# Mixture of experts in seven products a unit: P1 seeded into P2's bank by ScalarE, a second prefix added into P5's bank by VectorE, both gates read by silu from PSUM, down products in halves

## The reference

```python
# x: (16, 256, 256) float32; 8 routed experts and one shared; D = 256, F = 1024
g = einsum('bsd,edf->ebsf', x, Wg)
u = einsum('bsd,edf->ebsf', x, Wu)
expert_outs = einsum('ebsf,efd->ebsd', silu(g) * u, Wd)
expert_output = einsum('be,ebsd->bsd', probs, expert_outs)
shared = silu(x @ Sg) * (x @ Su) @ Sd
sg = shared_gate[:, None, None]
out = x + (1.0 - sg) * expert_output + sg * shared
```

## Time and profile before

| what | value |
|---|---|
| median of 3 runs | 2184.85 us (2184.4 to 2184.9) |
| the profiled execution's own time | 2184.52 us |
| its span (first to last instruction) | 2182.7 us |
| TensorE busy | 2157.2 us, 99% of the span, 9504 matmuls |
| VectorE busy | 1493.0 us, 68% |
| ScalarE busy | 1532.0 us, 70% |
| GpSimd busy | 1394.3 us, 64% |

### The profile page before, as it was taken

One profiled execution on the slowest core, in us unless ns is written; L12 is line 12 of the kernel. 1 busy time (PEld: TensorE's weight loads), 2 busy tenths in 40 slices (PEclk: granted clock), 3 DMA queues, 4 the chain that ended last, 5 costly groups with the idle time before them and its releaser, 6 DMA issues.

```text
span 2182.7 us, 34606 instructions
## 1 busy us (share of the span) xinstructions
PE 2157.2 (99%) x9504; PEld 1784.5 (82%) x9504; DVE 1493.0 (68%) x2622; ACT 1532.0 (70%) x2622; POOL 1394.3 (64%) x2055
## 2 busy tenths in 40 slices
PE   6999999999999999999999999999999999999998
PEld 5888888888888888888888888888888888888887
DVE  6666666666766666666676666666667666666666
ACT  6777677677777767766776776777677677777765
POOL 8766666666866666666686666666666666666662
PEclk9999999999999999999999999999999999999999
DMA  4111111111211111111121111111112111111110
GB/s 151 52 57 50 50 57 51 50 53 55 71 51 58 50 50 56 52 50 51 57 71 52 58 51 50 53 55 50 50 58 70 52 57 51 50 52 57 50 50 27
DMA packets 44171, 122.22 MB, mean 56 GB/s; under 512 B 4928, under 2 KB 4944, under 8 KB 44128
## 3 DMA queue, kind: packets, MB, share of 16 engines
q1 hardware_dynamic: 44064, 121.65, 18.3%
q0 software_dynamic: 64, 0.07, 0.1%
HBM read 117.51 MB, written 4.19 MB: 56 GB/s over the span
## 4 chain that ended last, share of the span: by engine, by line
PE 98%; DMA 0%; POOL 0%; ACT 0%; DVE 0%; issue 0%; SPq 0%; DVEq 0%; ACTq 0%
PE chain_ps L255 12%; PE down_ps L255 12%; PE chain_ps L257 12%; PE chain_ps L256 12%; PE down_ps L257 12%; PE down_ps L256 12%; PE p_ps L255 6%; PE p_ps L257 6%; PE p_ps L256 6%; PE p_up_ps L255 3%; PE p_up_ps L257 3%; PE p_up_ps L256 3%; DMA w_raw<-w 0%; POOL w_lo L183 0%; POOL w_raw L168 0%
## 5 line engine op out<-in xcount | busy, mean ns | idle before, releaser
L183 POOL TENSOR_TENSOR w_lo<-w_raw,w_hi 128x384 fp32r<-128x384 f32 x864 | 854.6, 1018 | 733.0 <-ACT w_hi L342 733.0
L168 POOL TENSOR_TENSOR w_raw<-w_raw 128x128 f32<-128x128 f32 x1152 | 509.6, 465 | 29.0 <-DMA w_raw<-w 6.4
L255 PE MATMUL chain_ps<-x_hi,w_hi 128*128 128x512 f32 x1152 | 449.1, 390 | 19.4 <-POOL w_lo L183 18.2
L342 ACT CAST w_hi<-w_raw 128x768 fp32r<-128x768 f32 x576 | 388.5, 675 | 86.9 <-PE down_ps L257 80.1
L255 PE MATMUL down_ps<-h_hi,w_hi 128*128 128x512 f32 x1152 | 448.3, 389 | 0.5 <-DVE h_lo L459 0.5
L256 PE MATMUL chain_ps<-x_lo,w_hi 128*128 128x512 f32 x1152 | 448.4, 389 | 0.0
L257 PE MATMUL chain_ps<-x_hi,w_lo 128*128 128x512 f32 x1152 | 448.4, 389 | 0.0
L257 PE MATMUL down_ps<-h_hi,w_lo 128*128 128x512 f32 x1152 | 448.1, 389 | 0.0
L256 PE MATMUL down_ps<-h_lo,w_hi 128*128 128x512 f32 x1152 | 448.1, 389 | 0.0
L363 ACT CAST h_hi<-p_up_ps 128x512 fp32r<-128x512 f32 x288 | 169.0, 587 | 307.0 <-DVE p_up_ps L451 307.0
L474 DVE TENSOR_TENSOR gate<-tap_p,p_up_ps 128x512 f32<-128x512 f32 x288 | 198.0, 687 | 248.6 <-PE p_up_ps L257 248.6
(11 more groups left out here) (46 smaller groups left out, 2852.6 us busy)
## 6 DMA issues: line engine op xcount, KB each, us to landing
w_raw<-w SPq DMA_DIRECT2D x288, 384.0 KB, 3.0
outT<-acc SPq DMA_DIRECT2D x8, 512.0 KB, 4.1
acc<-xT SPq DMA_DIRECT2D x6, 512.0 KB, 9.3
acc<-xT SPq DMA_DIRECT2D x4, 256.0 KB, 6.3
probs_sb<-probs POOLq DMA_DIRECT2D x1, 64.0 KB, 5.1
shared_sb<-shared_gate POOLq DMA_DIRECT2D x1, 8.0 KB, 6.3
```

Source lines behind the costliest of these rows:

```text
L168: nc.gpsimd.tensor_tensor(raw[:, cols(dst, dst)], raw[:, cols(a, a)], raw[:, cols(b, b)], op).then_inc(w_sums, 1)
L183: ins = nc.gpsimd.tensor_tensor(w_lo[:, s, c], w_raw[:, s, c], w_hi[:, s, c].bitcast(F32), ALU.subtract)
L255: nc.tensor.matmul(bank, w_hi[:, s, c], hi, start=start, stop=False, **on)
L342: nc.scalar.copy(w_hi[:, s, c], w_raw[:, s, c]).then_inc(w_hi_done, 1)
```

## The change

- ScalarE no longer copies P1 to SBUF (tap_p1). It copies it from the chain bank into the bank of P2 (now y_ps), and P2 is then accumulated on top by TensorE: the bank holds gate 0. The copy (the seed) waits until h1_lo(n-1) has read the bank, and P6(n) waits for the seed.
- One matmul ahead of all units opens that bank, so that later accumulating matmuls add to what ScalarE writes.
- gate0 and gate1 of VectorE and the tap of U2 are gone. In their place VectorE adds tap_p5 and U2 and writes the sum into P5's bank (now z_ps; `u4`, waits for P6 and the tap of P5), and P3 is accumulated on top: gate 1.
- Both silus read PSUM: silu 0 after P2, silu 1 after P3.
- up_of_1 waits for silu 0 instead of gate0; P5(n) waits for silu 1 of unit n-1.
- TensorE's order is now P4(n-1), P1(n), P5(n), first half of down0(n-2), P6(n), second half of down0(n-2), P2(n), P7(n), P3(n), down1(n-1). P7 waits for u4.
- ScalarE's order is now h1_hi(n-1), h0_hi(n-1), seed(n), tap of P5, weights' hi part 0, silu 0, weights' hi part 1, (casts of x), silu 1.
- VectorE's order is now h0(n-1), h1_lo(n-1), h0_lo(n-1), u4, up_of_1, h1(n), (add).

```diff
...
         warm = sb("warm", [P, 1])
 
         chain_ps = ctx.enter_context(nc.psum_tensor("chain_ps", [P, 2, TOKENS], F32))
-        p2_up1_ps = ctx.enter_context(nc.psum_tensor("p2_up1_ps", [P, TOKENS], F32))
-        p53_ps = ctx.enter_context(nc.psum_tensor("p53_ps", [P, TOKENS], F32))
+        y_ps = ctx.enter_context(nc.psum_tensor("gate0_up1_ps", [P, TOKENS], F32))
+        z_ps = ctx.enter_context(nc.psum_tensor("p5_gate1_ps", [P, TOKENS], F32))
         down_ps = ctx.enter_context(nc.psum_tensor("down_ps", [P, 2, DC, TOKENS], F32))
...
                     pe.wait_ge(x_lo_done, X_FORMS * g + form + 1)
                 return x_hi[:, g % 2, form, :], x_lo[:, g % 2, form, :]
 
-            def down0(k, start, stop):
-                for c in range(DC):
-                    last = product(
-                        down_ps[:, 0, c, :], k % SLOTS, D0 + c, h0_hi[:, k % 2, :], h0_lo[:, k % 2, :], start, stop
-                    )
-                last.then_inc(down_done[0], 1)
-
-            def down1(k, start, stop):
-                for c in range(DC):
-                    last = product(down_ps[:, 1, c, :], k % SLOTS, D0 + c, h1_hi[:], h1_lo[:], start, stop)
-                last.then_inc(down_done[1], 1)
+            def down0(k, c, start, stop):
+                last = product(
+                    down_ps[:, 0, c, :], k % SLOTS, D0 + c, h0_hi[:, k % 2, :], h0_lo[:, k % 2, :], start, stop
+                )
+                if c == DC - 1:
+                    last.then_inc(down_done[0], 1)
+
+            def down1(k, c, start, stop):
+                last = product(down_ps[:, 1, c, :], k % SLOTS, D0 + c, h1_hi[:], h1_lo[:], start, stop)
+                if c == DC - 1:
+                    last.then_inc(down_done[1], 1)
 
             def p4(g, k, n, first=False):
 
...
                 if not isinstance(n, int) or n > 0:
                     p4(g - 1 if first else g, (k - 1) % CHUNKS, n - 1, first=in_first and k == 1)
 
+                def down0_part(c):
+                    if not isinstance(n, int) or n > 1:
+                        opens = in_first and k == 2
+                        if c == 0:
+                            pe.wait_ge(h_lo_done[0], n - 1)
+                            if opens:
+                                after(pe, added[0], g)
+                        down0((k - 2) % CHUNKS, c, start=opens, stop=in_first and k == 1)
+
+                def down1_both():
+                    if not isinstance(n, int) or n > 0:
+                        pe.wait_ge(h_lo_done[1], n)
+                        opens = in_first and k == 1
+                        if opens:
+                            after(pe, added[1], g)
+                        for c in range(DC):
+                            down1((k - 1) % CHUNKS, c, start=opens, stop=first)
+
                 pe.wait_ge(w_lo_done, n + 1)
                 after(pe, h_lo_done[0], n - 1)
                 product(chain, s, A11, *x_of(g, B11, first), start=True, stop=True).then_inc(p1_done, 1)
-                after(pe, gate1_done, n)
-                product(p53_ps[:], s, S1, *x_of(g, T1, first), start=True, stop=True).then_inc(p5_done, 1)
-                if not isinstance(n, int) or n > 1:
-                    pe.wait_ge(h_lo_done[0], n - 1)
-                    opens = in_first and k == 2
-                    if opens:
-                        after(pe, added[0], g)
-                    down0((k - 2) % CHUNKS, start=opens, stop=in_first and k == 1)
-                pe.wait_ge(p1_tapped, n + 1)
+                after(pe, silu_done[1], n)
+                product(z_ps[:], s, S1, *x_of(g, T1, first), start=True, stop=True).then_inc(p5_done, 1)
+                down0_part(0)
+                pe.wait_ge(p1_seeded, n + 1)
                 product(chain, s, S2, *x_of(g, T2, first), start=False, stop=True, goes_on=True).then_inc(p6_done, 1)
-                after(pe, h_lo_done[1], n)
-                product(p2_up1_ps[:], s, A12, *x_of(g, B21, first), start=True, stop=True).then_inc(p2_done, 1)
-                pe.wait_ge(p5_tapped, n + 1)
-                product(p53_ps[:], s, S4, *x_of(g, B22, first), start=False, stop=True, goes_on=True).then_inc(p3_done, 1)
-                pe.wait_ge(u2_tapped, n + 1)
+                down0_part(1)
+                product(y_ps[:], s, A12, *x_of(g, B21, first), start=False, stop=True, goes_on=True).then_inc(p2_done, 1)
+                pe.wait_ge(u4_done, n + 1)
                 product(chain, s, S3, *x_of(g, T3, first), start=False, stop=True, goes_on=True).then_inc(p7_done, 1)
-                if not isinstance(n, int) or n > 0:
-                    pe.wait_ge(h_lo_done[1], n)
-                    opens = in_first and k == 1
-                    if opens:
-                        after(pe, added[1], g)
-                    down1((k - 1) % CHUNKS, start=opens, stop=first)
-
+                product(z_ps[:], s, S4, *x_of(g, B22, first), start=False, stop=True, goes_on=True).then_inc(p3_done, 1)
+                down1_both()
+
+            pe.wait_ge(x_lo_done, 1)
+            pe.wait_ge(w_lo_done, 1)
+            nc.tensor.matmul(y_ps[:], w_hi[:, 0, 0:P], x_hi[:, 0, B11, :], start=True, stop=True).then_inc(y_opened, 1)
             for g in range(GROUPS):
                 for k in range(CHUNKS):
                     unit(g, 0, k)
...
 
                 if not first:
                     h1_hi_of(n - 1)
+                    h0_hi_of(n - 1, k - 1)
                 act.wait_ge(p1_done, n + 1)
-                after(act, gate0_done, n)
-                nc.scalar.copy(tap_p1[:], chain_ps[:, k % 2, :]).then_inc(p1_tapped, 1)
+                if first:
+                    act.wait_ge(y_opened, 1)
+                after(act, h_lo_done[1], n)
+                nc.scalar.copy(y_ps[:], chain_ps[:, k % 2, :]).then_inc(p1_seeded, 1)
                 act.wait_ge(p5_done, n + 1)
                 after(act, up1_done, n)
-                nc.scalar.copy(tap_p5[:], p53_ps[:]).then_inc(p5_tapped, 1)
-                if not first:
-                    h0_hi_of(n - 1, k - 1)
+                nc.scalar.copy(tap_p5[:], z_ps[:]).then_inc(p5_tapped, 1)
                 if ahead:
                     weight_hi(n + AHEAD, (k + AHEAD) % SLOTS, 0)
-                act.wait_ge(p6_done, n + 1)
-                after(act, gate1_done, n)
-                nc.scalar.copy(tap_u2[:], chain_ps[:, k % 2, :]).then_inc(u2_tapped, 1)
+                act.wait_ge(p2_done, n + 1)
+                after(act, h0_done, n)
+                nc.scalar.activation(silu[:, 0], y_ps[:], ACT.Silu).then_inc(silu_done[0], 1)
                 if ahead:
                     weight_hi(n + AHEAD, (k + AHEAD) % SLOTS, 1)
                 if new_x:
                     for form in X_AT.get(k, ()):
                         x_form_hi(g + 1, form)
-                act.wait_ge(gate0_done, n + 1)
-                after(act, h0_done, n)
-                nc.scalar.activation(silu[:, 0], gate[:, 0], ACT.Silu).then_inc(silu_done[0], 1)
-                act.wait_ge(gate1_done, n + 1)
+                act.wait_ge(p3_done, n + 1)
                 after(act, h1_done, n)
-                nc.scalar.activation(silu[:, 1], gate[:, 1], ACT.Silu).then_inc(silu_done[1], 1)
+                nc.scalar.activation(silu[:, 1], z_ps[:], ACT.Silu).then_inc(silu_done[1], 1)
 
             act.wait_ge(warm_set, 1)
             nc.scalar.activation(warm[:], warm[:], ACT.Silu).then_inc(warmed, 1)
...
             def h1_lo_of(n):
                 dve.wait_ge(h_hi_done[1], n + 1)
                 after(dve, down_done[1], n)
-                nc.vector.tensor_tensor(h1_lo[:], p2_up1_ps[:], h1_hi[:].bitcast(F32), ALU.subtract).then_inc(
+                nc.vector.tensor_tensor(h1_lo[:], y_ps[:], h1_hi[:].bitcast(F32), ALU.subtract).then_inc(
                     h_lo_done[1], 1
                 )
 
-            def gate0(n):
-                dve.wait_ge(p2_done, n + 1)
-                dve.wait_ge(p1_tapped, n + 1)
-                after(dve, silu_done[0], n)
-                nc.vector.tensor_tensor(gate[:, 0], tap_p1[:], p2_up1_ps[:], ALU.add).then_inc(gate0_done, 1)
-
-            def gate1(n):
-                dve.wait_ge(p3_done, n + 1)
-                dve.wait_ge(u2_tapped, n + 1)
-                after(dve, silu_done[1], n)
-                nc.vector.tensor_tensor(gate[:, 1], tap_u2[:], p53_ps[:], ALU.add).then_inc(gate1_done, 1)
+            def u4(n, k):
+                dve.wait_ge(p6_done, n + 1)
+                dve.wait_ge(p5_tapped, n + 1)
+                nc.vector.tensor_tensor(z_ps[:], tap_p5[:], chain_ps[:, k % 2, :], ALU.add).then_inc(u4_done, 1)
 
             def up_of_1(n, k):
                 dve.wait_ge(p7_done, n + 1)
-                dve.wait_ge(p5_tapped, n + 1)
-                dve.wait_ge(gate0_done, n + 1)
-                nc.vector.tensor_tensor(p2_up1_ps[:], tap_p5[:], chain_ps[:, k % 2, :], ALU.add).then_inc(up1_done, 1)
+                dve.wait_ge(silu_done[0], n + 1)
```

(29 more changed lines are left out.)

## The result

| | before | after |
|---|---|---|
| median | 2184.62 us (4 runs) | 2339.45 us (4 runs) |
| the profiled execution's own time | 2184.52 us | 2339.39 us |
| its span | 2182.7 us | 2337.6 us |

The change makes the kernel slower: ratio 1.0708, 95% interval 1.0695 to 1.0721, 154.8 us. Forecast were 2322 us (+138), range 2290 to 2351.

The account below looks back on a forecast made before the run. TensorE, busy 99%, was taken as the bound. P6's wait for the seed (130.0 us), additions (3.2), address price (3.8) and start (1.0) summed to 138.0 on 2184.5: 2322 us, range 2290 to 2351.

Parts of the forecast that it names:

- links 1 to 3 and 6: From P4(n-1): h0 starts at 0.88 us, h1_lo 0.785 later, lasting 0.69; after the seed, ScalarE to TensorE takes 0.05.
- Link 4, VectorE to ScalarE: Hand-over from h1_lo's end on VectorE to the seed's start on ScalarE: 0.03 us.
- Link 5, the seed: The seed's copy on ScalarE, priced like the tap into SBUF: 0.589 us, with bounds 0.48 and 0.69.
- Link 7, the restart: TensorE restarts slowly after P6 was held: 0.14 us more per unit.
- The address price: h0, heading VectorE's queue, starts 0.12 us later once per loop pass for its changed coefficient address: 3.8 us.
- The additions: At changes of group the addition stands between h1 and h0 on VectorE: 6 times 0.54, 3.2 us.
- Start and tail: One opening matmul and less cover for P6 in the second unit: 1 us; the tail 0.
- The covers named: Work said to stay hidden: u4 by 0.4 us, up_of_1 by a us; T is the start of P4(n-1).
- The signs named: Profile after: P6 idle behind the seed, some 0.3 us on weight loads; unit 7.93; P7 not held; TensorE about 95%.
- not slower: Rival at P6's wait for the seed: chain 0.5 us shorter than its rows, so no cost, 2185 us; chance 2%.
- a smaller and a larger stall: Rivals at P6: links overlap at queue distance, 2268 us, 5%; seed at 0.69 and u4 late, 2380 us, 6%.
- The clock: Rival: TensorE's clock falls to its low level; a quarter of the units would give 2800 us; chance 1%.

Follow-up runs that it names:

- e1: The changed kernel with h1_lo ahead of h0 on VectorE and the seed ahead of h0_hi on ScalarE: 2197.64 us, ratio 1.0058.
- e9: The changed kernel with VectorE's and ScalarE's queues reordered, the seed's two waits swapped and the group-change additions moved later: 2190.39 us, ratio 1.0024.
- e8: The changed kernel with h0 as one 512-column instruction in place of two of 256: 2302.9 us, ratio 1.0541.
- e2: The changed kernel with h1_lo ahead of h0 on VectorE only, ScalarE's order kept: 2515.04 us, ratio 1.1509.
- e3: The changed kernel with the seed ahead of h0_hi on ScalarE only, VectorE's order kept: 2341.34 us, ratio 1.0714.
- e5: The changed kernel with the seed's two waits swapped, the one for h1_lo first and the one for P1 second: 2324.97 us, ratio 1.064.
- e4: The changed kernel with both halves of down0 ahead of P6: 2309.3 us, ratio 1.0568.

## Why the prediction was right, point by point

- **The bound and the sign**: right. TensorE had no slack to give, and e1 and e9, with all the change's accesses and no holds, come back to within 0.6 and 0.3% of before, not below it.
- **The chain, links 1 to 3 and 6**: right. 0.88, 0.785, h1_lo 0.685 and 0.05 stand in the timeline after as forecast; e8 shows by its size that h0 is on it, e1, e2 and e3 together that h1_lo's place behind h0 holds the seed, and h0_hi's would as soon as h1_lo is out of the way.
- **Link 4, VectorE to ScalarE**: mis-sized. 0.03 was taken from h1 to h1_hi; the seed needs 0.09, some 16 us over 287 units. e5 shows the order of its waits to be the cause in the ordinary units: 14.5 us.
- **Link 5, the seed**: 0.589 taken, 0.570 measured, 0.02 x 287 = 5 us the other way. The nearest row was a good one, and the bounds (0.48, 0.69) far too wide; the range drawn from them was wide enough to take in the misses of the other links, which it was not made for. By the Trainium skill (ScalarE: Activation LUTs, Step-by-step: what each stage is for) writing PSUM is the faster; the trace agrees, by 3%. But where the seed follows a copy into SBUF at queue distance, in e2, it takes 0.592, no less than the copies into SBUF there (0.591).
- **Link 7, the restart**: 0.14 taken from one case of the earlier trace rows, 0.15 on the average of the trace, some 3 us more.
- Together the links were taken as 0.453 a unit, and 0.495 was measured: 130.0 against 141.7. This term is most of the miss of 17 us. As they are written the links add up to only 0.446, 128 us (0.88 + 0.785 + 0.692 + 0.03 + 0.589 + 0.05 + 0.14 - 2.72), so the 0.453 is 2 us too high. With the three corrections (0.057 more, 0.019 less, 0.01 more) they give the measured 0.495. That the seed was shorter than taken hid a third of what the hand-over cost more.
- **The address price**: mis-sized. I took 0.12 once a pass, 3.8, and named twice that as its upper end. It is paid in two units of a pass, 0.125 each, 8.0 in all: the last h0 of a pass and the first of the next one, both issued in the next pass, start late behind P4. That the changed address is the cause is argued: the units of the written-out expert, at fixed addresses, don't have it (7.96 to 8.00 in the first unit of groups 2 to 4, as in ordinary units), but no run takes the register away by itself.
- **The additions**: 3.2 forecast, 3.9 found. **Start and tail**: 1.0 forecast, 1.2 found.
- **The covers named** (u4 under P7, silu 0, up_of_1, h1, the casts of the weights): all held, no wait of TensorE on them in the units. The first cast of the weights came at T + 4.81, as the 4.8 said; the step to it named the second down half 1.36 later in the order, and it is 0.68, the rest is the hold. That u4 is late next was right: e4 and e1 both run into it.
- **The signs named**: P7 not held and h1_lo 0.79 after h0 came as said; TensorE's busy share is 96%, not 95, and the weight loads stand 0.65 us a hold where some 0.3 were named.
- **The rivals**: not slower, a smaller and a larger stall, all fell with the trace. The clock: TensorE stood about 0.2 us between two recorded matmuls of each unit, and the granted clock stayed full in all 40 slices, as in the earlier trace rows, so that rival did not come. The Trainium skill (TensorE: Matmul & The Clock Gate, What's actually happening) has idling take the clock; no run here shows it taken once it was full.

## What to carry to other kernels

When a wait is added, find what stands ahead of the releaser in its own engine's queue, and ahead of that: here the seed needed h1_lo, h1_lo's queue had h0 in front, and h0 needed TensorE's own latest product, so the loop closed on the engine that bounds the kernel and each link of it counted one for one in 287 units. Less work on engines that are not the bound buys nothing; lay out the cover (how many matmuls TensorE has between the release and the need) beside the chain before moving either, and look at both queues together: here ScalarE's turned alone bought nothing, VectorE's alone cost 176 us more, and both gave back 142. Price the links from rows of the same engine pair with the same pattern of waits.

## What was not expected of the hardware

- The order of two waits ahead of one ScalarE instruction, both needed: 0.03 us from the releaser's end to the start when the later-satisfied stands first, 0.09 when it stands last; 14.5 us over the kernel (e5). In the first two units of a loop pass it is 0.107 and 0.087, the other way round.
- A copy of 128x512 from PSUM into PSUM takes 0.570 us where it starts on an idle ScalarE or after a gap, 0.592 at queue distance behind a copy into SBUF (e2).
- h0 starts 0.11 to 0.14 us later behind its waits in the first two units of a loop pass. That its register address, which has changed there, is the cause is argued and not shown.
